# The attention's output scratch laid out by tokens, and one load per chunk in the gate

## The reference, cut to what matters

```python
# x: 4 x 2048 tokens of 512 numbers; 16 heads of 32; windows of 128 tokens
x = x + layernorm(window_attention(layernorm(x), w_qkv))   # each window sees itself and both neighbours
y = layernorm(x)
h = relu(y @ gate_w1.T + gate_b1)
g = (h @ gate_w2.T + gate_b2).mean(axis=1)        # one row of 8 expert weights per sequence
mW1 = W1 + sum_e g[e] * TW1[e];  mW2 = W2 + sum_e g[e] * TW2[e]   # biases alike
x = x + layernorm(gelu(y @ mW1.T + mb1) @ mW2.T + mb2)
```

## Time and profile before

| | us |
|---|---|
| median of three runs | 3015.17 |
| the profiled execution, whole | 3024.29 |
| its span | 3022.5 |
| PE busy in the span | 2897.8 |
| attention's last store issued | 1307.3 |
| gate's first load issued | 1309.6 |
| first full product of the mixed network | about 1604 |

### The profile page before, as it was taken

One profiled execution on the slowest core, in us unless ns is written; L12 is line 12 of the kernel. 1 busy time (PEld: TensorE's weight loads), 2 busy tenths in 40 slices (PEclk: granted clock), 3 DMA queues, 4 the chain that ended last, 5 costly groups with the idle time before them and its releaser, 6 DMA issues.

```text
span 3022.5 us, 55745 instructions
## 1 busy us (share of the span) xinstructions
PE 2897.8 (96%) x20444; PEld 2421.8 (80%) x20444; DVE 1987.1 (66%) x3750; ACT 1727.5 (57%) x3384; POOL 841.6 (28%) x694
## 2 busy tenths in 40 slices
PE   7999999999999999949989999999999999999998
PEld 6888888788888888847777888888887888878886
DVE  4333333488777878757757776787669666786664
ACT  2222222366666767645545666776667666676665
POOL 1000000188888888753310000320005000040003
PEclk9999999999999999979999999999999999999999
DMA  5554555578877788669999776886569766796732
GB/s 189 186 180 167 180 191 199 192 190 190 192 182 187 194 193 197 161 206 359 360 347 358 268 244 204 322 341 234 203 215 390 258 213 216 277 366 215 242 133 84
DMA packets 388931, 697.07 MB, mean 231 GB/s; under 512 B 27192, under 2 KB 159288, under 8 KB 388680
## 3 DMA queue, kind: packets, MB, share of 16 engines
q1 hardware_dynamic: 368192, 646.15, 67.0%
q10 hardware_dynamic: 16416, 31.98, 3.0%
q0 software_dynamic: 4080, 15.73, 1.3%
HBM read 525.45 MB, written 167.78 MB: 229 GB/s over the span
## 4 chain that ended last, share of the span: by engine, by line
PE 45%; DMA 4%; DVE 3%; ACT 2%; issue 1%; SPq 1%; POOL 0%; POOLq 0%; DVEq 0%; ACTq 0%
PE e_hid L1243 7%; PE e_hid L1244 7%; PE e_hid L1245 7%; PE e_acc L1260 7%; PE e_acc L1262 7%; PE e_acc L1261 7%; DMA yl_scratch<-e_yt_lo 4%; DVE e_yt_lo L1504 1%; DVE e_c_stats L1477 1%; DVE e_part L1554 1%; DVE e_c_y L1498 0%; ACT e_sums L1375 0%; ACT e_yt_hi L1322 0%; PE e_hid L1224 0%; SPq L742 0%
## 5 line engine op out<-in xcount | busy, mean ns | idle before, releaser
L1554 DVE SCALAR_TENSOR_TENSOR e_part<-e_ring,e_g_cols,e_part 128x512 f32<-128x512 f32 x896 | 640.5, 772 | 3.8 <-DMA e_ring<-mix_rows 1.7
L466 DVE TENSOR_REDUCE a_neg_max<-a_ps_score 128x1 f32<-128x384 f32 (+1 forms) x1024 | 492.3, 527 | 69.3 <-PE a_ps_score L584 58.0
L311 POOL TENSOR_TENSOR a_total<-a_probs 128x512 f32<-128x512 f32 x256 | 323.9, 1281 | 622.6 <-ACT a_probs L396 622.6
L396 ACT ACTIVATE a_probs<-a_ps_keys 128x384 f32<-128x384 f32 (+1 forms) x1024 | 426.9, 478 | 58.7 <-PE a_ps_keys L601 31.0
L1358 ACT ACTIVATE e_u<-e_hid,e_mb 128x512 f32<-128x512 f32 x256 | 177.3, 693 | 445.6 <-PE e_hid L1245 439.5
L1578 DVE TENSOR_TENSOR e_u_lo<-e_u,e_u_hi 128x512 fp32r<-128x512 f32 x256 | 183.4, 716 | 315.4 <-ACT e_u_hi L1362 315.1
L1133 POOL TENSOR_SCALAR e_var<-e_moments 128x4 f32<-128x4 f32 x15 | 7.4, 491 | 1297.0 <-DVE e_moments L1590 1296.4
L601 PE MATMUL a_ps_keys<-a_q_st,a_k_st 97*128 97x384 f32 (+1 forms) x1024 | 315.2, 350 | 21.4 <-DMA a_q_st<-a_max_rows 20.2
L584 PE MATMUL a_ps_score<-a_k_st,a_q_st 96*128 96x384 f32 (+1 forms) x1024 | 329.3, 359 | 0.6 <-DVE a_neg_max L466 0.5
L321 POOL TENSOR_TENSOR a_total<-a_total,a_probs 128x512 f32<-128x512 f32 x224 | 286.1, 1277 | 71.8 <-ACT a_probs L396 69.2
L446 DVE TENSOR_TENSOR a_qk<-a_acc,a_qk 128x512 fp32r<-128x512 f32 x128 | 88.3, 690 | 316.8 <-ACT a_qk L352 316.7
(11 more groups left out here) (147 smaller groups left out, 6522.2 us busy)
## 6 DMA issues: line engine op xcount, KB each, us to landing
e_ring<-mix_rows SPq DMA_DIRECT2D x558, 512.0 KB, 5.2
qk_scratch<-a_qk SPq DMA_DIRECT2D x128, 512.0 KB, 3.0
a_k_st<-qk_scratch SPq DMA_DIRECT2D x180, 256.0 KB, 4.3
a_q_st<-qk_scratch SPq DMA_DIRECT2D x180, 256.0 KB, 4.2
a_x_in<-x SPq DMA_DIRECT2D x16, 1024.0 KB, 7.2
v_scratch<-a_v SPq DMA_DIRECT2D x64, 256.0 KB, 3.1
a_v_sb<-v_scratch SPq DMA_DIRECT2D x64, 256.0 KB, 4.9
o_scratch<-a_out SPq DMA_DIRECT2D x128, 128.0 KB, 3.1
```

What stands on the lines that cost most here:

```text
L311: add = pool.tensor_tensor(total[:, g % 2, i], p[0], p[1], ALU.add)
L396: act.activation(probs[:, m % PROBS, h, 0:(hi - lo) * WIN], ps_keys[x % TRIO][:, 0:(hi - lo) * WIN], ACT.Exp, scale=SCALE).then_inc(exp_do ...
L466: dve.tensor_reduce(neg_max[:, g % 2, i, h:h + 1], ps_score[y % TRIO][:, 0:(hi - lo) * WIN], AX_X, ALU.max, negate=True).then_inc(reduced, 1)
L1554: dve.scalar_tensor_tensor(out=part[:, n % 2, half, :], in0=ring[:, slot, :], scalar=g_cols[:, b, e:e + 1], in1=so_far, op0=ALU.mult, op1= ...
```

## The change

`o_dram` becomes [token, 512] with the 16 heads side by side. The store of a step writes 256 rows of 512 bytes as before, but the rows now lie 2048 bytes apart. The gate loads a chunk with one transfer of 1 MB, whose rows are 2 KB, in place of four of 256 KB; DVE waits for one transfer's count in place of four.

```diff
                 def store(g):
                     sp.wait_ge(norm_done, g + 1)
-                    dst = o_dram.rearrange("q t e -> (q t) e")[2 * WIN * g:2 * WIN * (g + 1), :].rearrange("(w p) e -> p w e", p=P)
+                    quad, at = divmod(2 * WIN * g, TOKENS)
+                    dst = o_dram[at:at + 2 * WIN, quad * QH * E:(quad + 1) * QH * E].rearrange("(w p) e -> p w e", p=P)
                     sp.dma_start(dst, out[:, g % 2]).then_inc(out_stored[g % 2], 16)
...
                def load(c):
-                    for q in range(QUADS):
-                        sp.dma_start(att[:, p, :, q * P:(q + 1) * P],
-                                     o_dram[q, rows, :].rearrange("(t p) e -> p t e", p=P)).then_inc(loaded[p], 16)
+                    sp.dma_start(att[:, p], o_dram[rows, :].rearrange("(t p) d -> p t d", p=P)).then_inc(loaded[p], 16)
...
                def take_stats(c, which):
-                        dve.wait_ge(loaded[p], 16 * QUADS * (c // 2 + 1))
+                        dve.wait_ge(loaded[p], 16 * (c // 2 + 1))
...
-    o_dram = scratch("o_scratch", [QUADS, TOKENS, QH * E])
+    o_dram = scratch("o_scratch", [TOKENS, D])
```

## The result

The kernel after took 3005.38 us in the median (2997.81 to 3015.47, 20 runs), the kernel before 3018.74 (3010.03 to 3036.36, 20 runs): a ratio of 0.9949, 95% interval 0.9939 to 0.996. By the ratio that is 15.4 us less (12.1 to 18.4), by the two medians 13.4, where 18.1 were forecast. The runs of before scatter by more than the change is worth, so single executions are compared here stage by stage and only the ratio tells the whole.

The account below looks back on a forecast made before the run. PE was taken to bound the attention and mixed network, transfers the gate. Steady part 16.1 plus start 2.0 made 18.1 us, from a 3015.2 us median to 2997; forecast's own range 2990 to 3004, widened to 2989 to 3009.

Parts of the forecast that it names:

- The gate is held by transfers: In the gate, DMA at 355 GB/s sets a 14.76 us period, where engines could keep 12.85.
- Rows of 2 KB give the time back: Gate's steady part: period falls from 14.76 to 13.3 us, eleven periods giving 16.1 us, ends 21.0 and 0.
- One issue in place of four: SP's queue in the gate: `yl` issued 3.5 us sooner, loop from 29.5 to 26.0 us; not a second gain.
- Start: Start of the gate: chunk 1's smaller wait and SP's sooner issue of x give 2.0 us, ends 0 and 3.5.
- Late part: From chunk 14's copy, behind expert weight loads, to the end: 0, with 1 us either way.
- The sum: Whole kernel: 16.1 us steady part plus 2.0 start, 18.1 us less, from a 3015.2 median to 2997.
- half a gain: Rival in the gate: both causes act, period 14.1, 8.8 us gained, 3006 us; 10%.
- The signs: Gate: copies 13.0 to 13.6 us, `yl_scratch` waits under 0.5, no packets under 2 KB, no slice below 350 GB/s.
- The store costs nothing: Attention's store with rows farther apart in DRAM: same transfers, issues and rows, so cost as before and no gain.
- The rule on 512 bytes as the rival: Gate's loads: 512 bytes already suffices for line rate, so the period would stay at 14.76 us.
- The first rival: Gate: small rows aren't the slowness, loads beside stores may be; only 0 to 3 us won, 3012 to 3015; 11%.
- The slower case: Attention: strided store takes 1.4 us more of all engines, 128 steps grow by 29 us, 3026 us; 5%.

Follow-up runs that it names:

- the run with the old layout and the old store, y first: Kernel before, with SP issuing the stores of y ahead of x1's store and the next load; period 14.41 us, ratio 0.9969 to before.
- the run with y first: Kernel after, with SP issuing the stores of y ahead of x1's store and the next load; period 12.88 us, ratio 0.9911 to the kernel before.

## Why the prediction was right, step by step

- *The gate is held by transfers.* Shown: with short rows the period is 14.75 us in the long run in either order of SP, and with long rows it falls.
- *Rows of 2 KB give the time back, a period of 13.3, 16.1 us.* Right in kind, too large: 13.72 and 11.46 us. I worked from the 400 GB/s of the stretch without short rows and added 0.2 for small waits. The term that was mis-sized is that margin: 0.87 us above the floor of 12.85, where I put 0.45.
- *One issue in place of four, "the loop by itself would go to 26.0 us".* This step failed. I let the landing of y stay as it was while its issue moved forward. It was issued 5.2 us sooner after x1's store (4.8 as against 10.0 us on the mean), more than the 3.5 I had, but took 14.3 us to land in the median, not 11.6. I read that as the same loads still queued ahead of it; no run separates this. The loop came to 27.4 us for two chunks (twice 13.72), not 26.0. I had written that this was the same gain seen from the queue; in fact it was the limit that was left, as the reordered run shows (12.88).
- *Start, 2.0 us.* 1.47, and 1.44 of it lies before chunk 1's statistics.
- *Late part, 0 within 1.* 1.59 us.
- *The sum:* 18.1 forecast; 14.5 in the gate by the profiles, 15.4 by the ratio. The late part, put at 0, makes up for 1.6 of the 4.6 us that the steady part falls short, which is luck. Of the time, 2997 forecast and 3005.4 measured, 3.6 us of the difference are the starting point (the kernel before took 3018.7 in the median of twenty runs, not 3015.2) and the rest the gain. 3005.4 lies outside the forecast's own 2990 to 3004 and inside the range only because that was widened for half a gain.
- *The signs.* Packets from 512 bytes to 2 KB are gone, and chunk 13's copy to the end takes 1494.0 us, not 1493.1. Three signs failed: the period is 13.72, not 13.0 to 13.6; waits for `yl_scratch` go up to 2.06 us; and slices of 179 and 205 GB/s remain, where none below 350 was to be. So slow slices are no mark of short rows by themselves, as I had read them in the earlier trace rows: with long rows the order of SP alone decides whether they are there.
- *The store costs nothing.* Borne out: landing 3.0 us, the main queue busy for 79.6% of 1000:1250 (78.8 before), PE's wait for the row maxima 13.4 us (13.9 before), and the gate's first load issued at 1301 to 1307 in all runs with it. The 5.5 us of the table above need no such cause: the run with the old layout and the old store, y first, issued its first load at 1303.29. The last row's +2.5 is of the same kind (1462.6 to 1470.0 among the runs whose code is the same from there on).
- *The rule on 512 bytes as the rival.* The Trainium skill, "DMA: Bandwidth & Descriptors", section Specifications, has 512 bytes as enough for line rate. The runs differ: with a fifth of the bytes in pieces of 512 bytes the stretch 1420:1500 moves 350 to 359 GB/s in six runs, and with all in rows of 2 KB 376 to 405 in five. The measurement decides.
- *The other rivals.* The first rival, that x's load or reads beside stores make the slow slices, is refuted by the run with y first, where x's load and the stores stay and a chunk's 5.24 MB move in 12.88 us, 407 GB/s (399 by the DMA view). Half a gain was put at a period of 14.1; 13.72 lies between that and the 13.3, at the edge of the forecast's 12.85 to 13.8, so something of that rival was true: a second cause, the order of SP, was left. The slower case didn't come.

## What to carry to other kernels

When a stage is held by DMA rate, look at the length of the unbroken pieces on both sides before the number of transfers: here 2048 pieces of 512 bytes cost at least 1.9 us more than the same megabyte in rows of 2 KB, of which the old order of issue let 1.0 be seen. Then look again at the order of issue on the queue: a store that frees a buffer belongs ahead of loads that are wanted two rounds later, and here that was worth nearly as much as the change itself: by the ratios both together give 27 us (20 to 34) and the change alone 15, and by the profiles the gate from its first load to chunk 15 goes from 250.3 to 235.8 us with the change and to 222.1 with both.

## What the runs showed of the hardware that was not expected

The profile's packet counts don't show the short pieces in every case. In the run with one issue and rows of 512 bytes in DRAM, the view of 1420:1500 has nearly all packets at 2 KB, yet the rate is that of the short rows; the second row below is of the run with short pieces in SBUF only.

```profile
DMA packets 14093, 28.04 MB, mean 350 GB/s; under 512 B 431, under 2 KB 431, under 8 KB 14088
```

```profile
DMA packets 22444, 28.22 MB, mean 353 GB/s; under 512 B 678, under 2 KB 11362, under 8 KB 22439
```

14093 packets with 431 under 2 KB move 350 GB/s, 22444 packets with 11362 under 2 KB move 353, and the kernel after, with 15529 packets in the same stretch, moves 386. So the count of packets doesn't tell the cost, and pieces of 512 bytes on either side bring it. Why they are slow, and what pieces of 1 KB cost below the bound of 0.8 us, stays open.

The busy share of the DMA engines doesn't tell either. In the stretch 1420:1500 it is 1.05 at 353 GB/s (old layout, y first), 1.04 at 386 (the kernel after) and 1.05 at 399 (y first), so a share of 1 did not mean that a stage had reached what the engines could move.
